# Experts' weights split into halves one stage earlier, kept in DRAM and loaded back, in a fused attention and mixture-of-experts kernel

## The reference, cut to what matters

```python
h = relu(x @ rW1 + rb1); h = relu(h @ rW2 + rb2)
scales = softmax(h @ rW3 + rb3)
topk_scales, topk_experts = top_k(scales, 2)          # capacity 10 tokens per batch and expert
hh = relu(einsum('ebnc,ech->ebnh', dispatched, eW1) + eb1)
eout = einsum('ebnh,ehc->ebnc', hh, eW2) + eb2
out = sum(topk_scales * gathered, axis=2)
```

## Time and profile before

| what | value |
|---|---|
| median of 3 runs | 2486.73 us (2481.61 to 2487.48) |
| the profiled execution, its own time | 2483.57 us |
| span of the profiled execution | 2482.0 us |
| PE busy | 95% of the span |
| DVE, ACT, POOL busy | 47%, 43%, 7% |
| mean granted clock of PE | 0.977 |

### The profile page before, as it was taken

The page is one execution under the profiler, slowest core; times in us unless marked ns, Lnnn a source line. Parts: engine busy times, 40 slices in busy tenths (PEclk is TensorE's granted clock), DMA queues, the critical chain, the costliest instruction groups (busy, mean ns, idle before and its releaser), DMA issues.

```text
span 2482.0 us, 51076 instructions
## 1 busy us (share of the span) xinstructions
PE 2360.9 (95%) x18944; PEld 1552.3 (63%) x18963; DVE 1176.5 (47%) x2305; ACT 1074.0 (43%) x2053; POOL 179.0 (7%) x256
## 2 busy tenths in 40 slices
PE   6999999998999799999999999999799999989997
PEld 2444688886878444444445888888344444457776
DVE  5553455446888453332322433333544445355553
ACT  3553445443666342332323333332345444457671
POOL 0000000003343000000000000000000000002123
PEclk9999999998999899999999999999899999989997
DMA  3330011102333231121110000001211111016663
GB/s 120 102 102 34 31 52 51 34 17 65 85 91 81 65 128 43 43 76 43 43 43 26 31 30 13 13 13 47 69 35 34 34 34 34 0 38 107 93 106 102
DMA packets 152205, 136.91 MB, mean 55 GB/s; under 512 B 93128, under 2 KB 135304, under 8 KB 145144
## 3 DMA queue, kind: packets, MB, share of 16 engines
q1 hardware_dynamic: 137804, 76.78, 12.0%
q0 software_dynamic: 10928, 55.60, 7.9%
q10 hardware_dynamic: 3324, 2.51, 0.3%
HBM read 90.80 MB, written 34.60 MB: 51 GB/s over the span
## 4 chain that ended last, share of the span: by engine, by line
PE 83%; ACT 5%; SPq 4%; DVE 4%; issue 2%; DMA 2%; POOL 0%; DVEq 0%; ACTq 0%; POOLq 0%
PE ps L694 31%; PE ps L711 25%; PE ps L955 13%; PE ps L1077 4%; PE ps L944 3%; PE ps L1065 3%; SPq L506 1%; DMA arena<-in_x 1%; SPq L505 1%; ACT arena L1225 1%; ACT misc L1226 1%; SPq L392 1%; PE ps L1101 1%; SPq L581 1%; PE ps L969 1%
## 5 line engine op out<-in xcount | busy, mean ns | idle before, releaser
L694 PE MATMUL ps<-xh,arena 128*128 (+1 forms) x5376 | 909.1, 312 | 18.4 <-DVE xh L1471 10.3
L711 PE MATMUL ps<-misc,arena 128*128 128x256 f16 (+1 forms) x4128 | 726.0, 312 | 8.9 <-DVE misc L1541 5.5
L694 PEld LDWEIGHTS ps<-xh,arena 128*128 (+1 forms) x5376 | 527.7, 98 | 290.5 <-issue 27.2
L711 PEld LDWEIGHTS ps<-misc,arena 128*128 (+1 forms) x4128 | 403.2, 98 | 222.0 <-issue 7.8
L1545 DVE SCALAR_TENSOR_TENSOR misc<-ps,misc 128x256 f16<-128x256 f32 (+1 forms) x480 | 255.0, 532 | 542.5 <-ACT misc L1158 541.7
L1158 ACT ACTIVATE misc<-ps 128x256 f16<-128x256 f32 (+1 forms) x480 | 225.0, 469 | 553.0 <-PE ps L694 553.0
L955 PE MATMUL ps<-arena 128*128 128x512 f16 x1536 | 336.7, 379 | 0.0
L955 PEld LDWEIGHTS ps<-arena 128*128 128x128 f16 x1536 | 148.2, 98 | 173.4
L1808 DVE TENSOR_TENSOR arena<-misc,arena 128x512 f16<-128x512 f32 x128 | 88.6, 692 | 229.4 <-ACT arena L1293 229.4
L1539 DVE TENSOR_TENSOR arena<-ps,misc 128x256 f32<-128x256 f32 (+1 forms) x208 | 105.2, 506 | 143.9 <-ACT misc L1154 143.1
L1154 ACT ACTIVATE misc<-ps 128x256 f32<-128x256 f32 (+1 forms) x208 | 93.5, 450 | 162.4 <-PE ps L694 161.7
(11 more groups left out here) (243 smaller groups left out, 2008.8 us busy)
## 6 DMA issues: line engine op xcount, KB each, us to landing
wstage<-in_m_w POOLq DMA_DIRECT2D x16, 1024.0 KB, 5.2
arena<-src_d SPq DMA_DIRECT2D x64, 256.0 KB, 3.7
src_d<-misc SPq DMA_DIRECT2D x24, 512.0 KB, 3.1
wstage<-in_c_wi POOLq DMA_DIRECT2D x6, 1024.0 KB, 5.5
wstage<-in_r_w POOLq DMA_DIRECT2D x5, 1024.0 KB, 5.3
cexp_d<-misc SPq DMA_DIRECT2D x18, 256.0 KB, 2.5
src_d<-misc SPq DMA_DIRECT2D x18, 256.0 KB, 2.5
cshare_d<-misc SPq DMA_DIRECT2D x8, 512.0 KB, 3.1
```

Of the source, the lines that this page charges most:

```text
L694: last = mm(ps[:, bank, col:col + p.n], weight(off, half, g, wp, k * F + f * 128), xh[:, xp, k, ds(start, p.n)], start=(k == 0 and n == 0) ...
L711: last = mm(ps[:, 4 + 2 * half + m, 0:p.n], weight(place[0], half, 2 if p.gated else 1, wp, f * D + m * 128), hid[:, st % 4, hp, 0:p.n], s ...
```

## The change

It does five things:

1. The 14 matrices of experts 1 to 7 (`loads[31]` to `loads[44]`) are split in `ee`, in 56 quarters ("pieces") of 512 columns, one at every 4th step from step 66 to step 286 of 288. High and low half go into one of two buffers (`piece`, in the area of `gt`, which `ee` does not use).
2. POOL stores each piece (256 KB) into a DRAM tensor `parts_d`, and fetches the next matrix after every fourth. ACT waits before a piece for the store of the piece two before, and before the router for all stores. POOL's `x1_back(0)` and `x1_back(1)` stand right behind the last piece instead of in expert 6.
3. The halves are loaded back from `parts_d`, 1 MB per matrix: those of expert 1 by SP when the router is done, those of experts 2 to 7 by DMAs that ACT issues at steps 4 and 5 of the expert before. PE waits for them (`mw_in0`, `mw_in1`) in place of `w_ready`.
4. In the experts the splitting is gone from ACT (28 x L1367) and DVE (28 x L1871).
5. The chain `eout` is spread: DVE's sum at steps 8, 9, 10 (and 1, 2) as before, ACT's high half one step later (9, 10, 11; and 2, 3), DVE's low half two steps after the sum (10, 11, 12; and 3, 4). `ev` alternates over all tiles. After the last expert DVE makes both sums before both low halves.

```diff
+        def piece_at(p, g):
+
+            n, rest = divmod(g - 66, 4)
+            return n if p is ee and not rest and 0 <= n < 8 * (NE - 1) else None
...
+            for n in range(8 * (NE - 1)):
+                pool.wait_ge(s["mw_lo"], n + 1)
+                pool.dma_start(parts_d[n // 4, :, :, (n % 4) * 512:(n % 4 + 1) * 512], piece[:, n % 2]
+                               ).then_inc(s[f"mw_st{n % 2}"], 16)
+                if n % 4 == 3 and FIRST_MOE + 2 + n // 4 < len(loads):
+                    fetch(FIRST_MOE + 2 + n // 4)
+
+            x1_back(0)
+            x1_back(1)
             for e in range(NE):
-                for i in range(FIRST_MOE + 2 * e + 2, min(FIRST_MOE + 2 * e + 4, len(loads))):
-                    fetch(i)
-                if e == NE - 2:
-                    pool.wait_ge(s["w_ready"], len(loads))
-                    x1_back(0)
-                    x1_back(1)
...
+            for u in range(2):
+                sp.wait_ge(s[f"mw_st{u}"], 64 * (NE - 1))
+            sp.wait_ge(s["l_mm"], 8)
+            for w in range(2):
+                slot = MOE_W[1][w]
+                sp.dma_start(arena[:, slot * SLOT:(slot + 1) * SLOT], parts_d[w].rearrange("p h n -> p (h n)")
+                             ).then_inc(s["mw_in1"], 16)
...
                 if st == 0:
-                    pe.wait_ge(s["w_ready"], e * 2 + FIRST_MOE)
+                    if e == 0:
+                        pe.wait_ge(s["w_ready"], FIRST_MOE)
+                    else:
+                        pe.wait_ge(s[f"mw_in{e % 2}"], 32 * ((e + 1) // 2))
...
+            def piece_high(n):
+
+                i, q = FIRST_MOE + n // 4, n % 4
+                if q == 0:
+                    act.wait_ge(s[f"w_in{i % 2}"], 16 * (i // 2 + 1))
+                if n >= 2:
+                    act.wait_ge(s[f"mw_st{n % 2}"], 16 * (n // 2))
+                fn(piece[:, n % 2, 0, :], wstage[:, i % 2, q * 512:(q + 1) * 512], ACT.Copy, scale=SW).then_inc(s["w_hi"], 1)
...
+            def expert_weights(e, w):
+
+                slot = MOE_W[e % 2][w]
+                act.wait_ge(s["m_out"], 2 * (e - 1))
+                act.dma_start(arena[:, slot * SLOT:(slot + 1) * SLOT], parts_d[2 * (e - 1) + w].rearrange("p h n -> p (h n)")
+                              ).then_inc(s[f"mw_in{e % 2}"], 16)
 
             def expert(e, fresh=False):
                 if fresh:
                     act.wait_ge(s["consts"], 1)
                 for st in range(16):
                     ehidden(e, st)
-                    if st in (1, 2) and not fresh:
-                        eout(e - 1, 1, (2 + st,))
-                    if st in (8, 9, 10):
-                        eout(e, 0, (st - 8,))
-                    if st in (2, 3, 5, 6) and e + 1 < NE:
-                        expert_weight_high(e, int(st >= 5), int(st in (3, 6)))
+                    if st in (4, 5) and not fresh and e + 1 < NE:
+                        expert_weights(e + 1, st - 4)
+                    if st in (2, 3) and not fresh:
+                        eout(e - 1, 1, (1 + st,))
+                    if st in (9, 10, 11):
+                        eout(e, 0, (st - 9,))
...
+            def piece_low(n):
+
+                i, q = FIRST_MOE + n // 4, n % 4
+                dve.wait_ge(s["w_hi"], 4 * i + q + 1)
+                last = v.scalar_tensor_tensor(piece[:, n % 2, 1, :], wstage[:, i % 2, q * 512:(q + 1) * 512], SW, piece[:, n % 2, 0, :],
+                                              ALU.mult, ALU.subtract)
+                last.then_inc(s["mw_lo"], 1)
...
+            def eout_sum(e, t):
+                dve.wait_ge(s["m_out"], e * 2 + (1 if t < 3 else 2))
+                if e * 5 + t >= 2:
+                    dve.wait_ge(s["eo_lo"], e * 5 + t - 1)
+                v.scalar_tensor_tensor(ev[:, (e * 5 + t) % 2, :], ps[:, 3 + t, 0:D], SEO / (SR * SW), misc[:, ds(e * D + 4608, D)],
+                                       ALU.mult, ALU.add).then_inc(s["ev"], 1)
+
+            def eout_low(e, t):
+                dve.wait_ge(s["eo_hi"], e * 5 + (t + 1))
+                v.tensor_tensor(eo[:, t, 1, :], ev[:, (e * 5 + t) % 2, :], eo[:, t, 0, :], ALU.subtract).then_inc(s["eo_lo"], 1)
...
+                    if st in (3, 4) and not fresh:
+                        eout_low(e - 1, st)
+                    if st in (10, 11, 12):
+                        eout_low(e, st - 10)
                     if st in (1, 2) and not fresh:
-                        eout(e - 1, 1, (2 + st,))
+                        eout_sum(e - 1, 2 + st)
                     if st in (8, 9, 10):
-                        eout(e, 0, (st - 8,))
-                    if st in (4, 5, 6, 7) and not lastone:
...
+                        eout_sum(e, st - 8)
```

More of the change, by code:

```diff
@@ L184, in build @@
         ev = misc[:, 2048:2048 + 2 * D].rearrange("p (u n) -> p u n", u=2)
+        piece = gt.bitcast(F16).rearrange("p (u h n) -> p u h n", u=2, h=2)
         turn_ps = ps[:, 7, :].bitcast(F16)
@@ L353, in build @@
         for e in range(1, NE):
-            wait = (s["l_mm"], 8) if e == 1 else (s["m_out"], 2 * (e - 1))
-            loads += [(a["m_w1"][e], MOE_W[e % 2][0], SW, wait), (a["m_w2"][e], MOE_W[e % 2][1], SW, wait)]
+            loads += [(a["m_w1"][e], None, SW, None), (a["m_w2"][e], None, SW, None)]
         PREP = {"cs": (0, 9, 6, 1), "ce": (9, 5, 2, 4), "s0": (14, 8, 4, 1), "s1": (22, 5, 4, 2), "s2": (27, 2, 4, 4),
@@ L1192, in body @@
                             weight_high(*piece)
+                        n = piece_at(p, i * 16 + st)
+                        if n is not None:
+                            piece_high(n)
                 body(0, True, False)
@@ L1328, in _ @@
             z_parts(1, 1)
+            for u in range(2):
+                act.wait_ge(s[f"mw_st{u}"], 64 * (NE - 1))
             router(0, True, True)
@@ L1376, in eout @@
                         act.wait_ge(s[f"eo_sp{t}"], e * 32)
[L1377 removed]
+                    fn(eo[:, t, 0, :], ev[:, (e * 5 + t) % 2, :], ACT.Copy).then_inc(s["eo_hi"], 1)
+            def expert_weights(e, w):
[3 more added lines that the diff above has]
+                              ).then_inc(s[f"mw_in{e % 2}"], 16)
             def expert(e, fresh=False):
@@ L1592, in body @@
                             weight_low(*piece)
+                        n = piece_at(p, i * 16 + st)
+                        if n is not None:
+                            piece_low(n)
                 body(0, True, False)
@@ L1840, in bias_scaled, with expert @@
                 link(v.tensor_scalar(misc[:, 4608:6656], misc[:, 4608:6656], SEO, None, ALU.mult))
-            def eout(e, half, tiles=None):
-                for t in (tiles or TILES[half]):
-                    dve.wait_ge(s["m_out"], e * 2 + (half + 1))
-                    if t >= 2:
-                        dve.wait_ge(s["eo_lo"], e * 5 + (t - 1))
-                    elif t == 0 and not (isinstance(e, int) and e == 0):
-                        dve.wait_ge(s["eo_lo"], e * 5)
-                    v.scalar_tensor_tensor(ev[:, t % 2, :], ps[:, 3 + t, 0:D], SEO / (SR * SW), misc[:, ds(e * D + 4608, D)],
-                                           ALU.mult, ALU.add).then_inc(s["ev"], 1)
-                    dve.wait_ge(s["eo_hi"], e * 5 + (t + 1))
-                    v.tensor_tensor(eo[:, t, 1, :], ev[:, t % 2, :], eo[:, t, 0, :], ALU.subtract).then_inc(s["eo_lo"], 1)
-            def expert(e, par, fresh=False, lastone=False):
+            def eout_sum(e, t):
[7 more added lines that the diff above has]
+                v.tensor_tensor(eo[:, t, 1, :], ev[:, (e * 5 + t) % 2, :], eo[:, t, 0, :], ALU.subtract).then_inc(s["eo_lo"], 1)
+            def expert(e, fresh=False):
                 for st in range(16):
@@ L1861, in expert @@
                         bias_scaled()
+                    if st in (3, 4) and not fresh:
+                        eout_low(e - 1, st)
+                    if st in (10, 11, 12):
+                        eout_low(e, st - 10)
                     if st in (1, 2) and not fresh:
-                        eout(e - 1, 1, (2 + st,))
+                        eout_sum(e - 1, 2 + st)
                     if st in (8, 9, 10):
-                        eout(e, 0, (st - 8,))
-                    if st in (4, 5, 6, 7) and not lastone:
-                        w, h = divmod(st - 4, 2)
-                        slot, cols = MOE_W[1 - par][w], slice(h * (MAT // 2), (h + 1) * (MAT // 2))
-                        dve.wait_ge(s["w_hi"], 4 * FIRST_MOE + e * 4 + (2 * w + h + 1))
-                        last = v.scalar_tensor_tensor(w16(slot, 1, h * (MAT // 2), MAT // 2),
-                                                      wstage[:, (FIRST_MOE + w) % 2, cols], SW,
-                                                      w16(slot, 0, h * (MAT // 2), MAT // 2), ALU.mult, ALU.subtract)
-                        if h:
-                            last.then_inc(s["w_ready"], 1)
-            expert(0, 0, fresh=True)
-            for e in range(1, NE - 1):
```

(11 more changed lines are left out.)

18 lines of the change are left out of this document (7 added, 11 removed).

## The result

| what | before | after |
|---|---|---|
| median of the runs | 2486.35 us (2481.61 to 2487.48, 4 runs) | 2524.52 us (2519.36 to 2526.51, 4 runs) |
| ratio, 95% interval | | 1.0154, 1.0136 to 1.0171 |
| span of the profiled execution | 2482.0 us | 2517.4 us |
| mean granted clock of PE | 0.977 | 0.971 |

The prediction was 2476.2 us, in a range of 2469 to 2489, faster with a chance of 0.63. The kernel became 38 us slower. Rival A, weights late, had been given 0.08 and priced at 2514 us.

The account below looks back on a forecast made before the run. PE was busy for 95% of the span, losing 1.68 us per expert to the output tiles' chain, and SP's store queue set the end. The terms -11.8 + 1.3 = -10.5 us gave 2476.2 us, range 2469 to 2489.

Parts of the forecast that it names:

- Rival A: Experts 2 to 7: ACT's weight loads late beside tile stores, 6.3 us wait each, 38 us, 2514 us; chance 0.08.
- The chain spread over steps: Experts 0 to 6, steps 9 to 11: PE's stall of 1.68 us per expert goes, 11.8 us gained.
- The last expert's tile 0: Expert 7's end: tile 0's low half comes later, so SP's last stores start later, costing 1.3 us.
- Splitting removed: Experts: 34.1 us of DVE and 29.9 us of ACT work gone, PE not waiting there; taken as 0.
- splitting added: Two-expert stage: 56 quarters on ACT and DVE hidden behind PE; taken as 0, high bound 17 us.
- POOL's stores: Two-expert stage: 56 piece stores and the matrix fetches have time enough on POOL; taken as 0.
- x1_back: Before the router: 2 MB moved behind the last piece; taken as 0, bounds 0 and 1.2 us, 3 for later loads.
- Loads back: Experts 1 to 6: ACT's two load issues hidden, loads land in time with 14.4 us left; taken as 0.
- The sum: Whole kernel: -11.8 + 1.3 = -10.5 us, forecast 2476.2 us.
- Against: the phase: Argument against Rival A: new loads start when stores of tiles 0 to 2 are through, DMA share 0.16.

Follow-up runs that it names:

- e1: The kernel before with only the output tiles' chain spread over steps, weights still split inside the experts: 2475.10 us, ratio 0.9954.
- e4: The kernel after with each tile store cut from 32 rows to 1 (32 KB to 1 KB), results incomplete: 2475.80 us in one run.
- e10: The kernel after with tile stores' 32 rows written into 32 partitions instead of one (last three tiles of expert 6 unchanged), values wrong: 2481.62 us, one run.
- e5: The kernel after with 14 unread matmuls on PE ahead of the weight waits of experts 2 to 7: 2521.57 us, ratio 1.0164.

## Why the prediction was wrong, step by step

*The chain spread over steps.* Right. The interval is 0.66 us at steps 9 to 11 in the kernel after, and e1 alone measures -10.4 us where the sum said -10.5 (with tile 0).

*The last expert's tile 0.* Right: +1.3 us said; SP starts 2.46 us after the end of out(7) (2460.55 - (2456.94 + 1.15)) where it was 1.40, +1.06. The queue ran a little faster (0.7 us), for which I had taken nothing.

*Splitting removed, splitting added, POOL's stores, x1_back.* All taken at 0, and right: up to the experts' first matmul the two spans differ by 0.07 us. The row of the two-expert stage has 2036 matmuls in 222 us, 9.17 per us, beside the 9.18 of the earlier trace rows:

```profile
1500.00:1722.00 222.00, 222.00 (x2036) 198.95 (x2034) 109.72 (x232) 94.30 (x224) 33.25 (x51) 1.00 0.31 105
```

*Loads back.* This step failed: "14.4 us are left ... The long ones were behind the stores of tiles 0 to 2; the new loads start when these are through (DMA share 0.16 ...). I take 0." The 14.4 us were nearly right. The second load was issued 6.1 us after out(0), so 21.9 - 6.1 = 15.8 us were left. It landed after 20.2 us, 4.4 too late, and that is the delay of 4.41 us in the timeline. (Beside the small stores of e4 these loads took 4.7 to 7.0 us, not far from the estimate of 4.4 us that the prediction took from the Trainium skill, DMA: Bandwidth & Descriptors, Anatomy of one DMA; the section gives that fit for DMAs issued by GpSimd, and these are ACT's.) The error was to price a load by the state of the engines at its issue. Over its whole flight it meets the stores of tiles 3 and 4 beside it and then those of tiles 0 to 2, which begin 10.6 us after it (2293.84). Three things in my own rows pointed there. The long landings up to 20.7 us were what a load costs that shares its flight with stores: in the trace before, the fetch issued at 2284.76 landed after 5.0 us, and the one at 2287.97, 1.7 us ahead of the first store of tiles 0 to 2 (2289.65), after 16.6. My 0.16 came from one window in the trace before, where the stores of tiles 3 and 4 had gone out 1.5 and 3.8 us after out(0); item 5 moves them to 4.2 and 6.1 us, so that they are in flight in that window, and I had moved the sums and copies without moving the stores that follow them. And a store of 32 KB with a median landing of 10 us, beside 2.5 us for one of 256 KB to DRAM, says by itself that it is no matter of bytes; I did not use that row (6.0 to 22.8 us, median 10.3, on L380 of the trace before).

*The slow steps behind a wait.* Not in the prediction, nor in rival A, which priced only the waits: six of 6.3 us, 38 us. Each of the six took 4.7 us of wait and 2.4 us behind it, 42.4 us together.

*The end.* +4.4 us between the start of the combine and the end, in no step. I had looked for effects only where the edits stand.

*The sum.* Without the late loads the stretch from experts to combine is 226.6 (e4) and 227.0 us (e10), against 238.06 - 10.5 = 227.6 by my sum. So all terms but one held within 1 us, and the one taken at 0 was worth +42.4 us. Rival A had the right mechanism and sign; what was wrong was its chance. That its 38 us lie near the 42.4 is in part luck: its waits were too long (6.3 us each, measured 4.7), and the slow steps behind them, which it did not have, made up for that. "Against: the phase" was one argument from one window against rows that showed 17.2 and 20.7 us.

## What to carry to other kernels

A transfer that is given a slack must be priced by all that shares the DMA engines from its issue to its landing, at the times that hold after the change: move the stores with the chain that feeds them, and take the long landings of the trace as the price until a row excludes them. Read landings against bytes: a small store that takes 10 us can hold engines that others need, and where it goes (one partition or many) can matter more than how much it carries. When a wait is for several semaphores, compare the landing of each with its end, and not only the name that the view gives. When an edit speeds up PE in a stage whose transfers are near their limit, take the two parts of the change apart; here one was worth -10 us alone, the other +17, and both together +38.

## What the runs showed of the hardware that I had not expected

- Many rows into one partition are dear: 32 KB stores of 32 rows land after 10.6 us at the median into one partition and after 2.2 us into 32, and 1 MB loads beside them after 14.1 us (up to 22.1) and 6.8 us (up to 8.6). The 1 KB packets of the stores took 173 and 46 ns at the median.
- The DMA share can stand at 1.07 to 1.21 with 38 to 63 GB/s moved. A high share says that packets take up the engines' time, not that they move much.
- After a wait of 4 to 6 us PE's next steps run at a granted clock of 0.50 and cost up to 2.7 us more; filling the wait with matmuls kept the clock behind the first wait but brought nothing in sum (e5).
- The stretch from combine to end is 4.3 to 4.4 us longer in every kernel where ACT issues the loads, and 56 more DMAs from POOL do not make it so. In the kernel after the extra time lies behind the last output store. The cause is open.
